# A table stage whose add moves to VectorE and whose steps are staggered, and relation weights made there instead of in the prologue

## The reference, cut to what matters

```python
h = relu(layernorm(x))
x = x + segment_sum(h[sender] * (softplus_shifted(edges @ W1 + b1) @ W2 + b2), receiver)   # filter layer
h = relu(layernorm(x))                                                                      # the table stage
W[r] = sum_b comp[r, b] * basis[b]                                                          # relation weights, for each of two layers
h1 = relu(mean over each type of h[src] @ W1[r] + h @ root1 + bias1)
x = x + (mean over each type of h1[src] @ W2[r] + h1 @ root2 + bias2)
```

## Time and profile before

| what | value |
|---|---|
| median of three runs | 7055.04 us |
| the profiled execution | 7061.2 us |
| its span, first to last instruction | 7059.4 us |
| TensorE busy | 72% of the span |
| VectorE busy | 61% |
| ScalarE busy | 31% |
| GpSimd busy | 76% |
| mean granted TensorE clock | 0.765 |

### The profile page before, as it was taken

The page is one execution under the profiler, slowest core; times in us unless marked ns, Lnnn a source line. Parts: engine busy times, 40 slices in busy tenths (PEclk is TensorE's granted clock), DMA queues, the critical chain, the costliest instruction groups (busy, mean ns, idle before and its releaser), DMA issues. The chain is left out here.

```text
span 7059.4 us, 123441 instructions
## 1 busy us (share of the span) xinstructions
PE 5114.7 (72%) x30996; PEld 4169.4 (59%) x30996; DVE 4282.4 (61%) x12408; ACT 2153.6 (31%) x4186; POOL 5343.6 (76%) x5119
## 2 busy tenths in 40 slices
PE   4887788788888877666666666666677777667777
PEld 3666666667777767555555555555455555545555
DVE  7677777667776665666666666666444444444444
ACT  4666666644444434222222222222100000000000
POOL 5777777788888885777777777777677777777776
PEclk9999999999999988666666666666666666666666
DMA  5776666599999876222222222222222222222222
GB/s 159 182 185 181 182 183 163 152 185 186 187 187 188 184 147 199 57 58 58 58 57 57 58 60 58 58 58 56 54 60 59 59 60 59 59 60 59 59 59 54
DMA packets 816671, 749.51 MB, mean 106 GB/s; under 512 B 127989, under 2 KB 719249, under 8 KB 815637
## 3 DMA queue, kind: packets, MB, share of 16 engines
q1 hardware_dynamic: 576676, 400.15, 22.3%
q0 software_dynamic: 237296, 340.25, 21.6%
q10 hardware_dynamic: 1974, 0.95, 0.1%
HBM read 574.58 MB, written 165.86 MB: 105 GB/s over the span
## 5 line engine op out<-in xcount | busy, mean ns | idle before, releaser
L2081 POOL DMA_INDIRECT got<-h_dram,etcol x3322 | 3208.0, 966 | 1043.6 <-issue 1016.7
L2208 DVE SCALAR_TENSOR_TENSOR hacc<-bank,hacc 128x256 f32 (+1 forms) x3322 | 1189.2, 358 | 1872.9 <-PE bank L2093 802.6
L2093 PE MATMUL bank<-share,got 128*128 128x128 f32 x4436 | 1095.5, 396 | 894.9 <-DMA got<-h_dram,etcol 843.3
L2093 PEld LDWEIGHTS bank<-share,got 128*128 128x128 f32 x4436 | 915.5, 278 | 1202.2 <-DMA got<-h_dram,etcol 1150.7
L1607 POOL DMA_INDIRECT msg_dram<-total,idx x1008 | 978.4, 971 | 332.4 <-issue 271.2
L1622 POOL DMA_INDIRECT acc_dram<-total,idx x653 | 1042.3, 1596 | 207.8 <-issue 196.9
L2093 PE MATMUL bank<-hot,got 128*128 128x128 f32 x2208 | 544.3, 395 | 432.3 <-DMA got<-h_dram,etcol 406.4
L2159 ACT ACTIVATE hacc<-ones_f 128x2048 f32<-128x2048 f32 (+1 forms) x196 | 290.8, 1484 | 1847.3 <-DVE umade L2231 1847.3
L2093 PEld LDWEIGHTS bank<-hot,got 128*128 128x128 f32 x2208 | 453.5, 277 | 586.5 <-DMA got<-h_dram,etcol 561.4
L2112 PE MATMUL bank<-wrel,umade 128*128 128x128 f32 x3136 | 689.1, 408 | 3.5 <-DVE umade L2231 3.4
L2189 DVE TENSOR_SCALAR share<-iota_f,dstcol 128x128 f32<-128x128 f32 x2218 | 661.1, 299 | 15.3 <-PEq L1646 8.1
(11 more groups left out here) (267 smaller groups left out, 8204.0 us busy)
## 6 DMA issues: line engine op xcount, KB each, us to landing
edges<-in_edge_attr SPq DMA_DIRECT2D x415, 256.0 KB
unit<-msg_dram SPq DMA_DIRECT2D x616, 129.0 KB
got<-h_dram,etcol POOLq DMA_INDIRECT x3322
low<-rows_dram SPq DMA_DIRECT2D x164, 256.0 KB, 4.3
win<-split_dram SPq DMA_DIRECT2D x416, 96.0 KB
low<-rows_dram SPq DMA_DIRECT2D x252, 128.0 KB, 4.3
acc_dram<-zeros SPq DMA_DIRECT2D x200, 128.0 KB
made<-acc_dram SPq DMA_DIRECT2D x147, 128.0 KB, 3.6
```

Of the source, the lines that this page charges most:

```text
L2081: pool.indirect_dma_start(got[k][:, j, :], None, g.h_dram[which][:, :], bass.IndirectOffsetOnAxis(ap=source[:, c:c + 1], axis=0)).then_inc ...
L2093: ins = nc.tensor.matmul(columns[j][:, 0:P], got[k][:, j, :], equal, start=True, stop=True)
L2208: v.scalar_tensor_tensor(to, columns[j].rearrange("p (a n) -> p a n", n=NARROW), 1.0, to, ALU.mult, ALU.add).then_inc(s_sum, 1)
```

## The change

1. `relation_term` and the loads of `comp` and `basis` leave the prologue. GpSimd there waits for four loads. SyncE issues the four others in the table stage, ahead of the loads of pair 4, and VectorE makes the weights there, one term of 128x128 in each of its steps 16 to 79, 64 in all.
2. TensorE sums only the four arrays. VectorE adds the bank to `xs`.
3. ScalarE makes relu(scale * xs + shift) in one activation. VectorE makes the shift, -mean * scale, for a pair at once; its two tensor_scalars of a pair go.
4. The wipe of the ring moves from VectorE to ScalarE, one 128x128 copy with scale 0 in each step.
5. The steps are staggered: VectorE makes in step s the add of block s, the statistics of block s-1, the shift of a pair (odd steps, pair (s-5)/2) and the aggregate of block s-2. ScalarE makes the logarithm and exponential in step 2q+3 and the relu of pair q in step 2q+6.
6. `own_gpsimd` is as it was.

```diff
-def relation_term(nc, chain, wrel, scaled, basis_sb, comp_sb, step):
...
+def relation_term(nc, wrel, basis_sb, comp_sb, n):
+
+    which, b, r = n // (NBASIS * R), n // R % NBASIS, n % R
+    to, of = wrel[which][:, r * F:(r + 1) * F], basis_sb[which][:, b, :]
+    rate = comp_sb[which][:, r * NBASIS + b:r * NBASIS + b + 1]
+    if b == 0:
+        return nc.vector.tensor_scalar(to, of, rate, None, ALU.mult)
+    return nc.vector.scalar_tensor_tensor(to, of, rate, to, ALU.mult, ALU.add)
...
-            pool.wait_ge(s_weights, 16 * 8)
+            pool.wait_ge(s_weights, 16 * 4)
...
-            for k in range(2):
-                for step in range(2 * NBASIS - 1):
-                    relation_term(nc, chain, g.wrel[k][:, :], scaled[:, :], basis_sb[k], comp_sb[k][:, :], step)
...
         def own_sync(sp):
             for q in range(PAIRS):
+                if q == 4:
+                    load_weights(sp)
                 need(sp, s_added, 2 * (q - 3))
...
-                nc.tensor.matmul(bank, g.ident[:, :], g.xs[:, b, :], start=True, stop=False)
                 for j in range(TG):
-                    ins = nc.tensor.matmul(bank, g.ident[:, :], loaded[q % 4][:, j, b % 2, :], start=False, stop=j == TG - 1)
+                    ins = nc.tensor.matmul(bank, g.ident[:, :], loaded[q % 4][:, j, b % 2, :], start=j == 0, stop=j == TG - 1)
...
-            for s in range(NBLK + 2):
-                if s >= 2 and s % 2 == 0:
-                    q = (s - 2) // 2
+            for s in range(NBLK + 6):
+                if s >= 3 and s % 2 and s - 3 < NBLK:
+                    q = (s - 3) // 2
                     act.wait_ge(s_var, 2 * q + 2)
-                    need(act, s_shift, 2 * (q - 1))
+                    need(act, s_shift, q - 1)
+                    need(act, s_h, 2 * (q - 1))
...
                 if s < NBLK:
-                    act.wait_ge(s_added, s + 1)
-                    nc.scalar.activation(g.xs[:, s, :], g.bank[s % 2][:, 0:F], ACT.Copy).then_inc(s_x, 1)
-                if s >= 3 and s % 2:
-                    q = (s - 3) // 2
+                    nc.scalar.activation(ring[:, s * P:(s + 1) * P], g.ones_f[:, :], ACT.Copy, scale=0.0)
+                if s >= 6 and s % 2 == 0 and s - 6 < NBLK:
+                    q = (s - 6) // 2
                     need(act, s_out[q % 4], q // 4 * 16)
+                    act.wait_ge(s_shift, q + 1)
+                    act.wait_ge(s_rstd, q + 1)
                     for b in range(2):
-                        act.wait_ge(s_shift, 2 * q + b + 1)
-                        nc.scalar.activation(rectified[q % 4][:, b, :], normed[q % 4][:, b, :], ACT.Relu).then_inc(s_h, 1)
+                        nc.scalar.activation(rectified[q % 4][:, b, :], g.xs[:, 2 * q + b, :], ACT.Relu, bias=shifts[q % 2][:, b, 0:1],
+                                             scale=scales[q % 2][:, b, 0:1]).then_inc(s_h, 1)
...
+            for s in range(NBLK + 6):
                 if s < NBLK:
...
+                    dve.wait_ge(s_added, s + 1)
+                    v.tensor_tensor(g.xs[:, s, :], g.xs[:, s, :], g.bank[s % 2][:, 0:F], ALU.add).then_inc(s_x, 1)
+                n = s - 16
+                if 0 <= n < TERMS:
+                    if n == 0:
+                        dve.wait_ge(g.s_weights, 16 * 8)
+                    if n >= R:
+                        dve.wait_ge(s_chain, n - R + 1)
+                    relation_term(nc, g.wrel, basis_sb, comp_sb, n).then_inc(s_chain, 1)
+                if 0 <= s - 1 < NBLK:
+                    b = s - 1
+                    dve.wait_ge(s_x, b + 1)
+                    need(dve, s_var, b - 1)
+                    v.bn_stats(moments[b % 2][:, :], g.xs[:, b, :]).then_inc(s_bn, 1)
+                if s >= 5 and s % 2 and s - 5 < NBLK:
+                    q = (s - 5) // 2
+                    dve.wait_ge(s_rstd, q + 1)
+                    need(dve, s_h, 2 * (q - 1))
+                    v.scalar_tensor_tensor(shifts[q % 2][:, :, :], norms[q % 2][:, :, 0:1], -1.0, scales[q % 2][:, :, :],
+                                           ALU.mult, ALU.mult).then_inc(s_shift, 1)
+                if 0 <= s - 2 < NBLK:
+                    b, q = s - 2, (s - 2) // 2
+                    dve.wait_ge(s_bn, b + 1)
                     need(dve, s_std, q - 1)
...
+                    need(dve, s_shift, q - 1)
+                    v.bn_aggr(norms[q % 2][:, b % 2, :], moments[b % 2][:, :]).then_inc(s_var, 1)
```

More of the change, by code:

```diff
@@ L179, in __init__ @@
         self.gate = nc.alloc_semaphore("gate")
+        self.s_weights = nc.alloc_semaphore("weights")
         NBX, NT, NG = self.NBX, self.NT, self.NG
@@ L354, in norm_variances, with prepare @@
     chain(nc.vector.tensor_tensor(g.shift[:, at], mean_e, mean_o, ALU.add))
-def relation_term(nc, chain, wrel, scaled, basis_sb, comp_sb, step):
[L359 to L368, removed]
+def relation_term(nc, wrel, basis_sb, comp_sb, n):
[5 more added lines that the diff above has]
+    return nc.vector.scalar_tensor_tensor(to, of, rate, to, ALU.mult, ALU.add)
+def prepare(nc, g, so, x, src, dst, edge_type, edge_attr, W1, b1, W2, b2, root, bias):
     N, E, NG, NBLK, NBX, QP, EQ = g.N, g.E, g.NG, g.NBLK, g.NBX, g.QP, g.EQ
@@ L439, in prepare @@
         bpart = sb("bpart", [P, F], BF16)
-        basis_sb = [sb(f"basis_sb{k}", [F, NBASIS, F]) for k in range(2)]
-        comp_sb = [sb(f"comp_sb{k}", [P, R * NBASIS]) for k in range(2)]
-        scaled = sb("scaled", [F, R * F])
         bn = sb("bn", [P, EARLY, 6])
@@ L453, in prepare @@
         s_x = sem("p_x")
-        s_weights = sem("p_weights")
+        s_weights = g.s_weights
         s_chain = sem("p_chain")
@@ L574, in _ @@
             act.dma_start(g.b1c[:, :], b1.rearrange("(f a) -> f a", a=1)).then_inc(s_weights, 16)
[L575 to L579, removed]
             def columns(turn, col):
@@ L1633, in _, with make_table @@
                 pool.wait_ge(s_sc[j], (NG if j < g.LASTJ else NG - 1) * 16)
-def make_table(nc, g, hacc):
+def make_table(nc, g, hacc, basis, comp):
     NBLK = g.NBLK
@@ L1670, in make_table @@
         seg = sb("seg", [P, g.NT])
+        basis_sb = [sb(f"basis_sb{k}", [F, NBASIS, F]) for k in range(2)]
+        comp_sb = [sb(f"comp_sb{k}", [P, R * NBASIS]) for k in range(2)]
+        TERMS = 2 * NBASIS * R
         s_low = sem("t_low")
@@ L1690, in make_table @@
         loaded = [made[k][:, :].rearrange("p (j b f) -> p j b f", j=TG, f=F) for k in range(4)]
-        normed = [sums[k][:, 0:2, :] for k in range(4)]
         rectified = [sums[k][:, 2:4, :] for k in range(4)]
@@ L1695, in make_table @@
         scales = [sb(f"tscales{k}", [P, 2, 1]) for k in range(2)]
+        shifts = [sb(f"tshifts{k}", [P, 2, 1]) for k in range(2)]
+        ring = hacc[:, :, :].rearrange("p b f -> p (b f)")
         low_b = seg
@@ L1699, in pair_rows, with load_weights @@
             return dram[q * 2 * P:(q + 1) * 2 * P, :].rearrange("(b p) f -> p b f", p=P)
+        def load_weights(sp):
+            for k in range(2):
+                sp.dma_start(comp_sb[k][:, :], comp[k].rearrange("r b -> (r b)").partition_broadcast(P)).then_inc(g.s_weights, 16)
+                sp.dma_start(basis_sb[k][:, :, :], basis[k].rearrange("b i o -> i b o")).then_inc(g.s_weights, 16)
         def own_sync(sp):
             for q in range(PAIRS):
+                if q == 4:
+                    load_weights(sp)
                 need(sp, s_added, 2 * (q - 3))
@@ L1766, in own_vector @@
             key = Chain(dve, s_key)
-            ring = hacc[:, :, :].rearrange("p b f -> p (b f)")
-            for s in range(NBLK + 2):
+            for s in range(NBLK + 6):
                 if s < NBLK:
[L1770 to L1775, removed]
-                    need(dve, s_std, q - 1)
[L1777 to L1785, removed]
+                    dve.wait_ge(s_added, s + 1)
[21 more added lines that the diff above has]
+                    dve.wait_ge(s_bn, b + 1)
+                    need(dve, s_std, q - 1)
+                    need(dve, s_shift, q - 1)
+                    v.bn_aggr(norms[q % 2][:, b % 2, :], moments[b % 2][:, :]).then_inc(s_var, 1)
@@ L1842, in step, with other_program @@
                     nc.tensor.transpose(g.bank[k][:, 0:P], h[k][:, :], g.ident[:, :]).then_inc(s_tr, 1)
-            if_own(pe, g, lambda: own_tensor(pe), lambda: blocks(pe, step))
+            def other_program():
+                pe.wait_ge(s_chain, 3 + TERMS)
+                blocks(pe, step)
+            if_own(pe, g, lambda: own_tensor(pe), other_program)
         @block.vector
@@ L1855, in segments @@
                 chain(v.tensor_scalar(g.srccol[:, :], seg[:, :], float(g.NROWS * R - 1), None, ALU.min))
+                dve.wait_ge(g.s_weights, 16 * 8)
+                for n in range(TERMS):
+                    chain(relation_term(nc, g.wrel, basis_sb, comp_sb, n))
             def step(s):
@@ L1999, in convolve @@
             bank_t, bank_left, bank_right, bank_own = g.bank[4], g.bank[5], g.bank[6], g.bank[7]
```

(1 more changed line is left out.)

6 lines of the change are left out of this document (3 added, 3 removed).

## The result

The changed kernel takes 7094.77 us (median of five runs, 7087.22 to 7098.09) against 7058.35 for the kernel before, a ratio of 1.0048, 95% interval 1.0035 to 1.006. It is slower by half a per cent; I had forecast 7053, range 7032 to 7078. A second set of runs gave 7085.11 against 7049.86, 1.0046 (1.0029 to 1.0062).

What follows compares the result with a forecast made beforehand. VectorE beside GpSimd was taken to bound the prologue, TensorE the table stage, with GpSimd's store-then-load order just behind. 7061.2 - 23.8 + 22 = 7059.4 us, or 7053 on the median's scale; range 7032 to 7078.

Steps and rivals of the forecast that it cites:

- Part 1: Prologue: moving the relation weights out ends VectorE's excess beside GpSimd and saves 23.8 us, bounds 20 to 26.
- Rival 3: Prologue: the saving is hidden by VectorE's waits for ScalarE, ids or x, leaving 7077 us; 8%.
- Part 2: Table stage: one matmul fewer, add on VectorE; TensorE's pair falls from 2.29 to 1.83 us and stops being the bound.
- Part 3: Table stage: the stagger makes GpSimd's loads wait on relu; three-pair lap 8.6 us, 2.88 a pair, 22 us lost.
- the lap's first term: Table stage, GpSimd's lap: TensorE's work on pair q+2, put at 1.83 us.
- rival 2: Table stage: TensorE falls to 1.2 GHz, a pair takes 3.40 us, total 7074 to 7090; 12%.
- the start: Table stage's first nine pairs, left as they are, bounds 5 us either way.
- the tail: End of the table stage (aggregate, exponential, relu, store), said to stay about 2.7 us.
- Rival 1: Table stage: DMA binds instead of the lap, 2.17 us a pair, -8 in all, total 7023; 17%.
- a second bound lies just behind: Table stage before the change: GpSimd issues a store, then a load, so a later relu is a later load.
- Clock mostly full: Sign that the forecast is right: TensorE's clock stays mostly full in the table stage.
- DMA near 75%: Sign that the forecast is right: DMA share in the table stage near 75%, against 94% before.

Runs made afterwards that it cites:

- second pair of profiles: The changed kernel and the kernel before, both unaltered, run and profiled again beside each other: medians 7085.11 against 7049.86 us.
- the prologue's half alone: Kernel before with relation weights moved (loads on SyncE, terms on VectorE), old add, relu and step order kept: 7038.92 us, ratio 0.998.
- late stores: Changed kernel with GpSimd storing six pairs behind its loads instead of four: 7023.26 us, ratio 0.9962.
- the load on SyncE: Changed kernel with each pair's fourth load issued by SyncE instead of GpSimd, stores still four behind: 7031.04 us.
- the old stage with the terms in it: Kernel before with relation weights moved; with late stores, six pairs behind instead of four, it took 7039.67 us, ratio 0.9984.

## Why the prediction was wrong

- **Part 1** held, and that its sum fits to 0.2 us is luck. The operations named gave 22.2 of the 22.3 us forecast (from 22.52 to 57.23 before, from 22.30 to 34.82 now). The ids' earlier arrival, for which I took 1.5, gave 0.2. Another 1.1 came behind, where VectorE waits for TensorE, and it was not in my sum. The second pair of profiles gave 20.8 in all, still within 20 to 26. Rival 3 (the saving is hidden) is out: the prologue's half alone made the kernel 14 us faster.
- **Part 2** held for TensorE's fast pairs only: at full clock a pair takes 1.8 to 1.9 us.
- **Part 3** named the right circle, and its length was right for a TensorE at full clock: 8.6 us forecast, and 9.0 and 8.6 us in the two turns at a granted clock of 1.00 (8.8 and 8.7 in two such turns of the second profile). **The step that failed** is the lap's first term, TensorE on pair q+2 at 1.83 us, the price at full clock. In most turns that pair ran at the slow clock, and the mean turn is 10.3 us (3 x 3.43). The turn from 2762.20 took 10.77, and against the forecast's terms it has: TensorE on its first pair 3.39 us, not 1.83 (+1.56); the two relus 0.87 us, not 0.55 (+0.32), as the activation that scales and shifts is longer than the plain one; landing 3.6, not 3.1 (+0.5; 3.3 is the median of the stretch). The rest of the chain took 0.24 less. Together 2.14. In the turn from 2695.90, the same chain, the first pair took 2.06 us and landing 3.2.
- The largest of these is rival 2, which I had kept as an alternative with 12%. It is no alternative: the circle makes the pauses, and from pair 8 on the seven bursts that stand behind pauses of 3.3 to 4.3 us take 7.1 to 8.5 us for three pairs, where three at full clock take 5.6. One behind a pause of 2.2 us was slow too, and those behind 0.6 to 2.8 us were otherwise fast; what tips a turn from one kind to the other is not shown. Windows over three bursts' first 3.4 to 4 us show the granted clock at 0.50 to 0.58, that is the level of 1.2 GHz for most of it, and 1.00 or 0.99 in the next 3.4 to 3.8 us of two of them:

```profile
2762.00:2766.00 4.00, 3.80 (x20) 3.83 (x21) 1.24 (x6) 0.00 (x0) 1.32 (x2) 0.58 0.41 146
2766.00:2769.40 3.40, 3.40 (x30) 3.23 (x29) 3.06 (x17) 2.42 (x10) 0.87 (x2) 0.99 0.53 157
```

```profile
2728.70:2732.10 3.40, 3.35 (x16) 3.38 (x17) 0.77 (x4) 0.00 (x0) 0.59 (x1) 0.53 0.46 149
2732.10:2735.90 3.80, 3.76 (x34) 3.56 (x32) 3.41 (x19) 2.50 (x11) 0.71 (x1) 1.00 0.49 140
2740.10:2744.00 3.90, 3.82 (x18) 3.85 (x19) 0.87 (x5) 0.00 (x0) 0.71 (x1) 0.50 0.27 96
```

- I had priced rival 2's pair at 3.40 us; the first pair of the burst took 3.39. Rival 2's 43 us for the stage, from 3.40 us for every pair, came out near the measured 43.4 by chance: only the first of three pairs runs slow, and the rest of its 3.43 a pair is waiting. I had the number and argued it away with a TensorE "busy without a break", which my own circle ruled out. By the Trainium skill, "TensorE: Matmul & The Clock Gate", section "HAM oscillation — how this bites in real kernels", a kernel that waits for DMA between bursts is slowed at each. The trace agrees for the seven bursts behind the longest pauses, and not for every burst: the turns from 2695.90 to 2713.49 us wait for their loads too and have a granted clock of 1.00.
- The pace was forecast as 2.88 us a pair (+0.57) and is 3.43 (+1.10): 21 of the missing 26 us. The rest is the start, +2.9 (inside my 5 us), and the tail, +2.0, which I had left unchanged.
- **Rival 1** (DMA bounds at 2.17 a pair) was the right answer to another question: it is what happens as soon as the circle is cut (2.14 with late stores, 2.27 with the load on SyncE), and its 7023 us is what the late stores gave.
- My reading of the kernel before, "a second bound lies just behind" in GpSimd's queue, stays open. Late stores gained nothing in the old stage with the terms in it, where a pair takes 2.5 us and not 2.33; they were not tried without the terms. "Clock mostly full" and "DMA near 75%" among my signs were wrong: 0.80 to 0.96 and 49 to 71%.
- The median lies 36.4 us above before where the two stages explain 24.7. The profiled pair has 8.3 more in the first relational layer, which the change does not touch and which other executions of the same kernels lack.

## What to carry to other kernels

Where a load stands behind a store in one queue, every step put between a sum and its store lengthens the load's circle; count in how many tiles the circle closes before staggering, and move the stores back by as many tiles as the stagger adds, or give loads a queue with no wait for results in it. If the forecast has TensorE pausing each turn, price the first work behind the pause at the slow clock as well. A swap of two instructions in an engine's list can be worth more than the instructions: here the place of one 0.29 us add was worth 23 us.

## What the runs showed of the hardware

- The two-array VectorE term takes 0.23 us (median of 48) in the old stage and 0.35 in the changed one, same form and line (L365), which is also what I had estimated for it; I didn't look for the cause of the difference.
- A ScalarE relu of 128x128 with scale and shift from two columns takes 0.87 us for two, the plain one 0.51 to 0.55.
- Three untouched stages vary by 6 to 13 us between executions (filter layer 10.3, first relational layer 13.3, second 6.5), so a difference of 8 us in an untouched stretch is no finding from one pair of profiles.
